# A graph network's message pass: one add moved to GpSimd, one gelu applied on the way out of PSUM, new engine orders

## The reference

```python
src, dst = (edge_index[0], edge_index[1])
edge_input = jnp.concatenate([x[src], edge_attr], axis=-1)
messages = _gelu(edge_input @ mW1 + mb1) @ mW2 + mb2
gates = jax.nn.sigmoid(_gelu(edge_input @ gW1 + gb1) @ gW2 + gb2)
aggregated = jax.ops.segment_sum(messages * gates, dst, num_segments=x.shape[0])
combined = jnp.concatenate([x, aggregated], axis=-1)
update = _gelu(combined @ uW1 + ub1) @ uW2 + ub2
h = x + update
mu = jnp.mean(h, axis=-1, keepdims=True)
var = jnp.mean(jnp.square(h - mu), axis=-1, keepdims=True)
return (h - mu) * jax.lax.rsqrt(var + 1e-05) * ln_g + ln_b
```

## Time and profile before

| | us |
|---|---|
| median of 3 runs (lowest, highest) | 11957.47 (11951.58, 11964.21) |
| profiled execution, its own time | 11956.96 |
| profiled execution, span of the trace | 11955.2 |
| mean granted TensorE clock of that execution | 0.738 |
| message pass, first gather to last VectorE instruction | 1889.9 to 2708.7 |
| 14 rounds, first gather to last | 3292.1 to about 10318 |

### The profile page before, as it was taken

The page is one execution under the profiler, slowest core; times in us unless marked ns, Lnnn a source line. Parts: engine busy times, 40 slices in busy tenths (PEclk is TensorE's granted clock), DMA queues, the critical chain, the costliest instruction groups (busy, mean ns, idle before and its releaser), DMA issues. The chain is left out here.

```text
span 11955.2 us, 140496 instructions
## 1 busy us (share of the span) xinstructions
PE 6883.6 (58%) x20977; PEld 4313.5 (36%) x20977; DVE 6471.5 (54%) x24207; ACT 4318.2 (36%) x14541; POOL 8488.0 (71%) x8647
## 2 busy tenths in 40 slices
PE   4687677975655556556565565555556555672000
PEld 4566566664433323323333332333323323352000
DVE  6577896898844444444444444444444444575444
ACT  5698566877722222222222222222222222373000
POOL 6675765536777777777777777777777777776777
PEclk7665667877777777777777777777777777896555
DMA  7998885668854444444444444444444444473221
GB/s 246 304 251 239 267 276 150 188 182 271 259 152 140 118 115 116 114 114 117 113 118 114 114 116 114 118 113 114 118 114 117 113 115 118 150 233 123 64 66 55
DMA packets 1059890, 1804.54 MB, mean 151 GB/s; under 512 B 515278, under 2 KB 525948, under 8 KB 1059661
## 3 DMA queue, kind: packets, MB, share of 16 engines
q1 hardware_dynamic: 777325, 1384.14, 34.9%
q0 software_dynamic: 282336, 418.19, 16.1%
HBM read 1070.12 MB, written 738.89 MB: 151 GB/s over the span
## 5 line engine op out<-in xcount | busy, mean ns | idle before, releaser
L351 POOL DMA_INDIRECT r_g<-y_t,idx_s x5768 | 5545.6, 961 | 1984.6 <-issue 1856.9
L1895 DVE SCALAR_TENSOR_TENSOR F<-r_g,scan_s,F 128x96 f32<-128x96 f32 x5488 | 1769.4, 322 | 3981.9 <-DMA r_g<-y_t,idx_s 3088.0
L1995 PE MATMUL r_pu<-r_S,ident 128*128 128x384 f32 x2688 | 1734.2, 792 | 2803.7 <-DVE r_S L1897 2803.7
L2023 ACT ACTIVATE H<-r_pu,kc_e 128x96 f32 (+1 forms) x5474 | 1340.3, 355 | 5542.5 <-PE r_pu L1995 5508.8
L1995 PEld LDWEIGHTS r_pu<-r_S,ident 128*128 128x128 f32 x2688 | 678.5, 278 | 3553.5 <-DVE r_S L1897 3219.8
L1897 DVE SCALAR_TENSOR_TENSOR r_S<-r_S,scan_s,r_g 128x96 f32<-128x96 f32 x5488 | 1716.3, 313 | 0.0
L1977 PE MATMUL r_pu<-H,ident 128*128 (+2 forms) x2744 | 1530.5, 649 | 93.4 <-DMA r_c<-c_t 87.8
L1978 PE MATMUL r_pu<-r_c,ident 128*128 128x384 f32 (+1 forms) x2744 | 1347.3, 579 | 0.0
L1977 PEld LDWEIGHTS r_pu<-H,ident 128*128 128x128 f32 x2744 | 776.4, 284 | 766.8 <-issue 656.9
L1978 PEld LDWEIGHTS r_pu<-r_c,ident 128*128 128x128 f32 x2744 | 666.8, 243 | 560.9 <-issue 361.9
L2282 PE MATMUL e_pc<-e_S,B 128*128 128x96 f32 x2 | 0.7, 474 | 1050.9 <-DVE e_o L2326 1050.9
(11 more groups left out here) (329 smaller groups left out, 12095.3 us busy)
## 6 DMA issues: line engine op xcount, KB each, us to landing
r_c<-c_t SPq DMA_DIRECT2D x686, 384.0 KB
y_t<-H SPq DMA_DIRECT2D x672, 384.0 KB
r_g<-y_t,idx_s POOLq DMA_INDIRECT x5880, 2.5
kv_t<-n_kv SPq DMA_DIRECT2D x49, 776.0 KB, 6.7
y_t<-d_yx SPq DMA_DIRECT2D x98, 384.0 KB
agg_t<-e_S SPq DMA_DIRECT2D x49, 416.0 KB, 4.5
x1s_t<-e_xb SPq DMA_DIRECT2D x50, 384.0 KB, 4.9
h_t<-e_h SPq DMA_DIRECT2D x50, 384.0 KB, 5.3
```

The lines of the kernel that those rows point to most:

```text
L351: G.indirect_dma_start(out=to(j), out_offset=None, in_=table, in_offset=bass.IndirectOffsetOnAxis(ap=idx_s[:, h, j:j + 1], axis=0)).then_i ...
L1895: own.add(V.scalar_tensor_tensor(out=F[:, 0:D], in0=g[:, j, :], scalar=scan_s[:, h, j, 1:2], in1=F[:, 0:D], op0=ALU.mult, op1=ALU.add))
L1995: last = T.matmul(pu[h % 2][g][:], ident[:], S[:, h % 2, 4 * g:4 * g + 4, :], start=False, stop=True)
L2023: last = A.activation(v[:, j, :], pu[h % 2][j // 4][:, j % 4, :], ACT.Copy, scale=k[:, j, 0:1])
```

## The change

In the message pass:

- `hidden`, the add of 128 x 768 into `e_ur`, goes from VectorE to GpSimd, behind the gathers of the batch six later.
- The gelu of 128 x 768 in SBUF is gone. TensorE transposes the sum itself, and ScalarE applies gelu while it takes the transpose out of PSUM, in place of the copy.
- The lists of all five engines are written in a new order, with some other lags: the normalisation's second half and the store come one to two ticks earlier, the store of the sums one tick later.

In the rounds, `r_c` gets four buffers for two, and its load runs three batches ahead for one. To make room, the weights and `dst_i` are put into memory that is given back before the rounds.

```diff
+                    def hidden(b, n, h):
+                        after(pool, s_s, b + 1)
+                        pool.wait_ge(s_u[h], 16 * (n + 1))
+                        after(pool, s_ta, 2 * b - 2)
+                        G.tensor_tensor(ur[:, h % 2], S[:, h], u0[:, h % 2], ALU.add).then_inc(s_pr, 1)
+                        if isinstance(b, int) and b == NB - 1:
+                            first_rows()
...
-                    skewed(pool, (0, step))
+                    skewed(pool, (0, edges_only(step)), (6, hidden), total=NX)
...
-                    def gelu(b, n, h):
-                        after(act, s_pr, b + 1)
-                        A.activation(ur[:, h % 2], ur[:, h % 2], ACT.Gelu).then_inc(s_gr, 1)
-
-                    def gelu_turned(g):
+                    def gelu_u(g):
...
-                            A.copy(uT[0:D, h % 2, g, :], pu[0:D, :]).then_inc(s_ut, 1)
+                            A.activation(uT[0:D, h % 2, g, :], pu[0:D, :], ACT.Gelu).then_inc(s_ut, 1)
...
-                    skewed(sp, (6, load_u), (16, store), (0, edges_only(load)), (9, load_h1), (11, load_xb),
-                           (7, edges_only(store_sums)), total=NX)
+                    skewed(sp, (6, load_u), (14, store), (0, edges_only(load)), (9, load_h1), (10, load_xb),
+                           (8, edges_only(store_sums)), total=NX)
...
-                    skewed(dve, (10, scale), (11, update), (6, hidden), (9, add(1)), (9, add(0)), (9, stats),
-                           (5, gated(1)), (12, norm2), (5, gated(0)), (11, stats2), (5, total), total=NX)
+                    skewed(dve, (6, total), (9, add(1)), (10, scale), (11, norm2), (9, add(0)), (9, stats),
+                           (5, gated(0)), (10, update), (5, gated(1)), (10, stats2), total=NX)
...
-            cs = sb("r_c", [P, 2, J, D], F32, p6)
+            cs = sb("r_c", [P, K, J, D], F32, p6)
...
-                            after(sp, s_up, r * NB + b - 1)
+                            after(sp, s_up, r * NB + b - 3)
...
-                        skewed(sp, (1, store), (-1, load))
+                        skewed(sp, (1, store), (-3, load))
```

More of the change, by code:

```diff
@@ L273, in program, with weight @@
         weight_loads = []
-        def weight(name, parts, width, rows=D + 1):
-            t = sb(name, [rows, width])
+        def weight(name, parts, width, rows=D + 1, ctx=None):
+            t = sb(name, [rows, width], ctx=ctx or nodes)
             for r0, r1, c0, c1, a in parts:
@@ L285, in col @@
             return v.rearrange("(n a) -> n a", a=1)
+        w_3 = weight("w_3", [(0, D, 0, D, W3)], D, D, outer)
+        r_rows = weight("r_rows", [(0, 1, 0, D, row(ln_g)), (0, 1, D, 2 * D, row(ln_b)),
+                                   (0, 1, 2 * D, 3 * D, row(b3))], 3 * D, 1, outer)
+        r_all = sb("r_all", [P, 3, D])
+        nodes = outer.enter_context(ExitStack())
+        dst_i = sb("dst_i", [P, CH], I32, nodes)
         w_kvq = weight("w_kvq", [(0, D, 0, D, Wk), (0, D, D, 2 * D, Wv), (0, D, 2 * D, 3 * D, Wq),
@@ L301, in program @@
         c_u1 = weight("c_u1", [(0, D, 0, 1, col(ub1))], 1, D)
-        r_rows = weight("r_rows", [(0, 1, 0, D, row(ln_g)), (0, 1, D, 2 * D, row(ln_b)),
-                                   (0, 1, 2 * D, 3 * D, row(b3))], 3 * D, 1)
-        w_mu = sb("w_mu", [D + 1, D])
-        r_all = sb("r_all", [P, 3, D])
-        nodes = outer.enter_context(ExitStack())
+        w_mu = sb("w_mu", [D + 1, D], F32, nodes)
         iroot = sb("iroot", [P, CHS], F32, nodes)
@@ L1363, in step, with first_rows @@
                         gathers(h1_t, lambda j: xe[:, h, j, ED:ED + D], h, s_g[h])
-                    skewed(pool, (0, step))
-                    for h in range(K):
-                        pool.wait_ge(s_ss[h], 16 * OF[h])
-                    G.indirect_dma_start(out=Z[:, 0:D], out_offset=None, in_=agg1_t,
-                                         in_offset=bass.IndirectOffsetOnAxis(ap=idx_f[:], axis=0)
-                                         ).then_inc(s_single, 16)
+                    def hidden(b, n, h):
[5 more added lines that the diff above has]
+                            first_rows()
+                    def first_rows():
+                        for h in range(K):
+                            pool.wait_ge(s_ss[h], 16 * OF[h])
+                        G.indirect_dma_start(out=Z[:, 0:D], out_offset=None, in_=agg1_t,
+                                             in_offset=bass.IndirectOffsetOnAxis(ap=idx_f[:], axis=0)
+                                             ).then_inc(s_single, 16)
+                    skewed(pool, (0, edges_only(step)), (6, hidden), total=NX)
                 @block.tensor
@@ L1409, in carry, with turn_hidden @@
                             T.matmul(pm[:, 0:D], B[:], S[:, h, J - 1, :], start=True, stop=True).then_inc(s_cr, 1)
-                    def turn_gelu(g):
+                    def turn_hidden(g):
                         def run(b, n, h):
-                            after(pe, s_gr, b + 1)
+                            after(pe, s_pr, b + 1)
                             after(pe, s_ut, 2 * b + g)
@@ L1434, in hidden_g @@
                         return edges_only(hidden(g, pg, w_g1, s_pg, s_gt))
-                    skewed(pe, (3, hidden_m(0)), (7, turn_gelu(0)), (3, hidden_g(0)), (3, hidden_m(1)),
-                           (3, hidden_g(1)), (4, edges_only(message(1))), (2, edges_only(turn(0))),
-                           (4, edges_only(message(0))), (2, edges_only(turn(1))), (8, outer_layer(1)),
-                           (7, turn_gelu(1)), (8, outer_layer(0)), (6, edges_only(carry)), total=NX)
+                    skewed(pe, (2, edges_only(turn(0))), (3, hidden_g(0)), (3, hidden_m(0)),
+                           (4, edges_only(message(0))), (3, hidden_g(1)), (2, edges_only(turn(1))),
+                           (7, turn_hidden(0)), (3, hidden_m(1)), (8, outer_layer(1)), (7, turn_hidden(1)),
+                           (8, outer_layer(0)), (4, edges_only(message(1))), (6, edges_only(carry)), total=NX)
                 @block.scalar
@@ L1543, in total @@
                         (first_sums if isinstance(b, int) and b == NB else sums)(b, n, h)
-                    def hidden(b, n, h):
-                        after(dve, s_s, b + 1)
-                        dve.wait_ge(s_u[h], 16 * (n + 1))
-                        after(dve, s_ta, 2 * b - 2)
-                        V.tensor_tensor(ur[:, h % 2], S[:, h], u0[:, h % 2], ALU.add).then_inc(s_pr, 1)
                     def add(g):
@@ L1970, in start @@
                                 pe.wait_ge(s_h[h], 16 * (n + 1))
-                            pe.wait_ge(s_c[h % 2], 16 * (r * PER[h % 2] + 2 * n + h // 2 + 1))
+                            pe.wait_ge(s_c[h], 16 * (r * OF[h] + n + 1))
                             after(pe, s_s, r * NB + b - 1)
@@ L1977, in start @@
                                 T.matmul(to, ident[:], cols(H, b)[:, c, :], start=True, stop=False)
-                                T.matmul(to, ident[:], cs[:, h % 2, c, :], start=False, stop=False)
+                                T.matmul(to, ident[:], cs[:, h, c, :], start=False, stop=False)
                         def add(b, n, h):
```

20 lines of the change are left out of this document (9 added, 11 removed).

## The result

The changed kernel takes 12016.08 us (median of 5 runs, 12012.22 to 12019.53), the kernel before 11952.9 us beside it. The ratio is 1.0057, with a 95% interval from 1.0045 to 1.0069. Forecast were 11923 us and at most 11972. Two later pairs of the same kernels gave 1.0057 [1.0041, 1.0074] and 1.0058 [1.0042, 1.0073].

What follows compares the result with a forecast made beforehand. VectorE was taken to bound the message pass. 33 us less from its pace, 3 more at the start, 4 less at the end and 0 in the rounds gave -34 us: 11923 us, 8-in-10 range 11892 to 11972.

Steps and rivals of the forecast that it cites:

- The pace: Message pass: a tick of 14.0 us instead of 14.77, over 43 ticks 33 us less.
- The bound's reading: Message pass before the change: VectorE bounds it, its own chain of 14.18 us being 96% of the 14.77 us tick.
- VectorE loses the add: VectorE in the message pass: 0.88 us a tick less, so its own tick becomes 13.3 us.
- ScalarE's part: ScalarE in the message pass: 1.93 us less work a tick, most of VectorE's 0.5 us waits for roots gone.
- GpSimd's add: GpSimd in the message pass: the add takes 2.0 us (0.68 as other end), making its tick 13.5 us.
- What it costs the others: Message pass: GpSimd's add disturbing VectorE, with remaining ScalarE waits and a longer TensorE wait, costs 0.5 us a tick.
- the first rival: Message pass: GpSimd's add holds VectorE's small scale 1.25 us each tick, no change, 11953 us; chance 0.26.
- GpSimd as the bound: Message pass: GpSimd's add, held and slowed by VectorE, makes its tick 15.4 us, time 11990 us; chance 0.13.
- The start: Start of the message pass: first ticks delayed about 10 us by seven batches of gathers, mostly made good, +3 us.
- The end: End of the message pass: adds -1.8 us, earlier last update and norm -6, stall for the stored sums +4, together -4.
- The rounds: The rounds, with GpSimd's gathers setting their pace: four r_c buffers change 0 us, between -5 and +5.

Runs made afterwards that it cites:

- e10_fill: e9_gate_act with six batches of gathers instead of seven ahead of GpSimd's first add, and a 128x1 GpSimd add in the phase before: 11938.6 us, ratio 0.9984.
- e4_more: The kernel before with the add on GpSimd, gelu out of PSUM and four r_c buffers, other engines' orders unchanged; on a quick chip: 11984.54 us, ratio 1.0025.
- e9_gate_act: The changed kernel with gated(0) right behind the sums, outer_layer(1) ahead of message(0), four e_ur buffers and tanh(0) earlier on ScalarE: 11955.59 us, ratio 0.9997.

## Why the prediction was wrong

*The pace is the step that failed.* The prediction took it as the larger of two engines' own chains (13.3 and 13.5) "with 0.5 on top: 14.0 us". It was 16.30. What it left out is a loop through both engines, from VectorE's add(1) over gated(0) to TensorE's message(0) and outer_layer(1) and back. The change puts four steps instead of one between message(0) and outer_layer(1) on TensorE (7.4 us for 2.2 to 4.2), and GpSimd's add holds the scale between add(1) and gated(0) on VectorE (7.2 us for 6.0). The four steps are the same work in another place, and free on TensorE itself; together with the hold they stretch a loop of some 10 to 12.5 us to 16.5, and it passes both engines' own chains. Opening it at one place takes 42 us away, and opening it on both engines, with the buffers and the tanh, brings 14.36, in reach of the forecast 14.0. Counted over the right 42 ticks, the forecast pace would have been 47 us less and not 33; the measured one is 49 more.

*The bound's reading* was right in kind and wrong by a count: the mean tick is 15.12 us, so what the loops between engines added was 0.94 us above the shortest tick, not 0.59. The engine "at 96%" was one at 94%, so orders had more to give or to take than the prediction thought. TensorE's 561 us are 13.3 us a tick by the right count, not 13.0.

*VectorE loses the add*: right, and its own chain became the 13.3 us that were forecast. In e10_fill the last tick is 13.83 us, VectorE waits for nobody in it, and 0.54 of it are a held scale (0.71 us for 0.17), which leaves 13.29:

```profile
2595.66 2.77 DVE L1536 SCALAR_TENSOR_TENSOR e_S<-e_S,scan_s,e_g 128x96 f32<-128x96 f32 x8
...
2599.63 0.71 DVE L334 SCALAR_TENSOR_TENSOR e_rn<-e_mv,e_rn 128x8 f32<-128x8 f32 x1
...
2609.49 2.76 DVE L1536 SCALAR_TENSOR_TENSOR e_S<-e_S,scan_s,e_g 128x96 f32<-128x96 f32 x8
```

*ScalarE's part* was right: two table loads a tick, busy 459.5 us in a longer stretch for 534. The waits for roots fell from 22.7 us to 8.4 in the same 680 us, and it helped nothing, since ScalarE then waited 221 us for TensorE.

*GpSimd's add* took 1.81 us, under the 2.0 taken. The estimate from the Trainium skill's figure ("GPSIMD Engine Reference", section 3.1), scaled to 768 elements, was 1.7 us; the trace is 7% above it.

*What it costs the others* was sized at 0.5 us a tick, with everything else that might be left in it. The held scale alone is 1.27 - 0.17 = 1.10 us, near the first rival's 1.25 and twice the 0.5. That rival named the instruction, the mechanism and the sign in the profile ("over a microsecond"), and they came true; its price of 11953 did not, as it too had no loop. Its reason for the meeting was only partly right: the add began with TensorE's release (192.1 us of its waits) and not with the end of the sums (12.5). The rule of the Trainium skill ("SBUF — State Buffer", "Who interferes with whom") holds in these traces in both directions: VectorE's eight columns ended with GpSimd's add, and GpSimd's add took 2.59 us beside VectorE's in e4_more.

*GpSimd as the bound* did not occur: its adds waited 214.0 us in all.

*The start* was +3 and is +20.7: 5.1 up to the first sums and 15.6 up to batch 6. "Most of it is made good" was wrong already by the count: the early ticks took 76.5 / 6 = 12.8 us and not 15.3, less than GpSimd's 13.5, so there was nothing to make it good with. The first use of the add on GpSimd, 7.3 us, was in no row. Delay and first use go with the fill's repair (78.1 for 76.6), apart from the 5 us ahead of the first sums, which come with the new orders (39.8 us in e4_more, 44 in the others) and were not taken apart.

*The end* was -4 and is +1.0. *The rounds* were 0, and are: 1.0006 with an interval that holds 1. The 7.6 us less in the changed kernel's profile is no more than such profiles differ (7574.9 to 7601.8 us over all kernels).

What stays open: the share of the new orders without GpSimd's add on a quick chip, since all three runs of that kernel fell on the other kind; how much of TensorE's part of the loop is its low clock and how much the four steps; and what makes the slower chips slower.

## What to carry to other kernels

When a change reorders several engines, follow each bank or buffer that two of them share once round the tick, from release to release, and add up what stands between on both. The longest such loop is a bound beside every engine's own chain, and no busy share shows it. A sign here was that all three crowded engines were further from full while the tick grew; one instruction moved on one engine then tells more than any change of work. Moving an elementwise step to an idle engine that shares VectorE's way to SBUF saved here only what it did not hold, and where it landed depended on what released it, which the number of buffers can change.

## What the runs showed of the hardware that was not expected

- The first tensor_tensor on GpSimd started 6.8 to 7.6 us late with nothing to wait for, whether of 128x768 or of 128x1, and no later one did.
- An instruction of 128x8 with two SBUF operands on VectorE took 1.27 us on the mean for 0.17 beside GpSimd's add, and up to 2.25 us (e4_more). The adds out of PSUM (L1557) stayed as they were, 551 ns after and 546 before.
- On ScalarE a tanh straight behind a root loads a table, and the gelu behind it another (2312.47 and 2313.96 us in e10_fill's timeline, 1.28 us each), while behind a gelu the tanh needs none. With the third load a tick (e9_gate_act) the pace still fell, from 14.79 to 14.36 us.
- The same kernel takes 11964 us on one chip and 14052 on another: the kernels that ran on both kinds are 17 to 18% slower there, and orders that lose on the quick chips against the kernel before (outer_layer(1) earlier, 1.0025) win there (0.9937). Which of two versions is better depended on the chip.
